# Two-layer graph network on one core: one-hots of rows and columns made two steps ahead, and 40 gathered blocks in layer 1 instead of 46

## The chip, the cores and the metric

One core of one Trainium2 chip runs the whole program. The metric is the device time of one execution in microseconds (us). The five engines are named as in the profile: PE (TensorE, with its weight loads as PEld), DVE (VectorE), ACT (ScalarE), POOL (GpSimd) and SP (SyncE, which only issues DMAs here).

## The reference

The graph has 12500 nodes of 128 features and 412500 edges (`src`, `dst`, a type of 0 or 1), sorted by `dst`. Each of two layers normalizes and rectifies the nodes, sums neighbours' rows by destination, multiplies by small weights and adds the result to `x`.

```python
h = jnp.maximum(_layernorm(x), 0.0)
# layer 0: m = h[src] @ W.T + b, W and b by the edge's type
x = x + relu(segment_sum(m, dst) + (h @ W_self.T + b_self))
h = jnp.maximum(_layernorm(x), 0.0)
# layer 1
agg = segment_sum((h @ W_in.T)[src], dst)
deg = segment_sum(1, dst)
x = x + agg + deg[:, None] * (h @ W_out.T)
```

## The kernel before

The kernel sums rows of `h` first and multiplies by the weights afterwards. A row of `h` is held as three bf16 parts (`RW` = 384 columns). Nodes are in `NB` = 98 blocks of 128; edges, sorted by destination, lie in tiles of 128. The sum for a block of destinations is made in one of two ways. The first `GATHERED[l]` blocks of layer l are gathered, the others, `D` of them, are dense.

A **gathered** block: for each tile of 128 edges POOL issues one indirect DMA that brings the 128 source rows from the table in HBM into `rows` (L578). DVE makes the one-hot matrix of destinations for a group of `GROUP` = 5 tiles (`make_hot`, L1128), and PE multiplies rows by one-hots into `bank_g` (`add_group`, L665). `rows` holds `RINGS` = 3 groups, so POOL waits for `s.added` of the group three before.

A **dense** block: the adjacency counts of 128 (layer 1) or 64 (layer 0) destinations against all 98 blocks of sources are built in 16 steps. In each step DVE makes a one-hot of source rows and one of source columns for a few edge slots of each destination (`mark`, L1140 and L1142), PE multiplies them (`build`, eight matmuls, L717) into `bank_m`, and ACT copies that pair of banks into the adjacency (`built`, two copies, L958) before PE may build the next step. Meanwhile PE multiplies the adjacency of the block before with the table in SBUF, 98 matmuls of 384 columns, 6 or 7 in a step (`dense`, L732). The edges of a dense block come by one indirect DMA from `pk` (POOL, L563), are unpacked on DVE (`unpack`, L1152 to L1175) and turned on PE (L683, L684). Layer 0 does this for all its 98 blocks, since it also counts edges so; layer 1 for its dense blocks only.

Each engine runs through the same loop over steps `s_` in program order, and `Plan` says what lies in which step. A layer has `S = 16 * (Q + 1)` steps for its Q dense units (Q = D in layer 1, 2 D in layer 0), and the groups are spread evenly over them:

```python
self.due = [8 + g * (self.S - 12) // self.groups for g in range(self.groups)]
```

Within one step PE adds the groups that are due, turns and finishes blocks (L675, L692, L705, L706), builds, and does its dense part; DVE makes the hots of groups due up to three steps later, then one pair of marks, then the rest of its work. The two one-hot buffers `is_row` and `is_col` are used in turn, and `mark` for step s+1 waits until both halves of the build of step s-1 are done (`s.built`). POOL does not run by steps: its queue is just the gathers in order, with the `pk` DMAs between the groups. Layer 1 starts when every block of layer 0 is stored (`s_stored`); SP then loads the new table into SBUF.

Of the kernel before, what the change touches and what calls it, by code (L numbers as in the profile page):

```python
# [4 lines left out]
P = 128  # L5


def gnn_kernel(nc, x, src, dst, etype, w_data, b_data, w_ctrl, b_ctrl, w_self, b_self, w_in, w_out, out):
    fp32, bf16, i32, i16 = mybir.dt.float32, mybir.dt.bfloat16, mybir.dt.int32, mybir.dt.int16
# [6 lines left out]
    NB = -(-N // P)  # L16
# [20 lines left out]

    GATHERED = (NB * 29 // 49 // 2 * 2, NB * 23 // 49 // 2 * 2)  # L40
    KINDS = (2, 1)
    GROUP, RINGS = 5, 3
    PACKS = 4


    WIN, LEAD = 96, 46
# [20 lines left out]
    class Plan:  # L67


        def __init__(self, l):  # L70
            self.G = G = GATHERED[l]
            self.D = NB - G
# [76 lines left out]
    with ctx:  # L149
        def sb(name, shape, dt):  # L150
            return ctx.enter_context(nc.sbuf_tensor(name, shape, dt))

        def pb(name, shape, dt=fp32):
            return ctx.enter_context(nc.psum_tensor(name, shape, dt))

        def sem(name):
            return ctx.enter_context(nc.semaphore(name))
# [15 lines left out]
        ROWS_AT = 2 * A_W  # L173
        HOT_AT = ROWS_AT + RINGS * GROUP * RW // 2
        R_AT = HOT_AT + RINGS * GROUP * WIN
        C_AT = R_AT + 2 * 4 * P // 2
        CW = max(2 * NC0, 4 * NC1)
        PACK_AT = C_AT + 2 * CW // 2
        V_AT = PACK_AT + PACKS * 3 * P
        E_AT = V_AT + 3 * HALF  # L180
        GE_AT = E_AT + HALF
# [6 lines left out]
        arena = sb("arena", [P, max(D16_AT + (T + 1) // 2, RC_AT + 4 * P)], fp32)  # L188
# [9 lines left out]
        adj1 = [a.rearrange("p (c d) -> p c d", d=P) for a in adj]  # L198
        rows = arena[:, ROWS_AT:HOT_AT].bitcast(bf16).rearrange("p (t c) -> p t c", c=RW)
        hot = arena[:, HOT_AT:R_AT].bitcast(bf16).rearrange("p (t c) -> p t c", c=2 * WIN)  # L200
        is_row = arena[:, R_AT:C_AT].bitcast(bf16).rearrange("p (k n r) -> p k n r", k=2, n=4)
        is_col = arena[:, C_AT:PACK_AT].bitcast(bf16).rearrange("p (k c) -> p k c", k=2)
        pack = arena[:, PACK_AT:V_AT].rearrange("p (k c) -> p k c", k=PACKS)
        mine = arena[:, V_AT:E_AT].rearrange("p (k s) -> p k s", k=3)
        slot = arena[:, E_AT:GE_AT].bitcast(i32)
# [13 lines left out]

        ident = sb("ident", [P, P], fp32)  # L220
        ident_b = sb("ident_b", [P, P], bf16)
        ones = sb("ones", [P, 1], fp32)
        ones_b = sb("ones_b", [P, 1], bf16)
        eps = sb("eps", [P, 1], fp32)
        offset = sb("offset", [P, 1], fp32)
        base_g = sb("base_g", [P, 1], fp32)
        wT = sb("wT", [P, 5, F], fp32)
        bias = sb("bias", [P, 3, F], fp32)
        count = sb("count", [P, 3, NB], fp32)
# [4 lines left out]
        tmax = sb("tmax", [P, CH], fp32)  # L234
        tmin = sb("tmin", [P, CH], fp32)
        worst = sb("worst", [P, 4], fp32)
        missed = sb("missed", [P, 1], fp32)
        covered = sb("covered", [1, 1], i32)
        root = sb("root", [P, 1], fp32)


        SG_AT = 0
# [30 lines left out]
        shift = arena2[:, LN_AT + 4 * NB:LN_AT + 5 * NB]  # L273
        st1 = sb("st1", [P, 6], fp32)
        mv1 = sb("mv1", [P, 2], fp32)
        std1 = sb("std1", [P, 1], fp32)
        rstd1 = sb("rstd1", [P, 1], fp32)
        shift1 = sb("shift1", [P, 1], fp32)

        def stat_col(c, a, b):  # L280
            return stats.rearrange("p (n c) -> p n c", c=6)[:, a:b, c]
# [4 lines left out]
        bank_m = [pb(f"bank_m{k}", [P, 512]) for k in range(2)]  # L286
# [6 lines left out]
        iota_r = iota_ps[:, 0:P]  # L293
# [47 lines left out]
        for l in range(2):  # L341
            s = Layer()
# [3 lines left out]
            s.pair_out = sem(f"l{l}_pair_out")  # L346
            s.pack = [sem(f"l{l}_pack{k}") for k in range(PACKS)]
            s.unpacked = sem(f"l{l}_unpacked")
# [145 lines left out]
        def _(pool):  # L494
# [60 lines left out]
            def fast(l):  # L555
# [3 lines left out]
                def fetch(i):  # L559
                    if i >= PACKS:  # L560
                        pool.wait_ge(s.unpacked, i - PACKS + 1)
                    m = plan.fetch[i][1]
                    pool.indirect_dma_start(  # L563
                        out=pack[:, i % PACKS, :], out_offset=None, in_=pk,
                        in_offset=bass.IndirectOffsetOnAxis(ap=list_at[:, m:m + 1], axis=0),
                        compute_op=ALU.bypass).then_inc(s.pack[i % PACKS], 16)
# [45 lines left out]
        def _(pe):  # L612
            pe.wait_ge(s_ident, 2)
            pe.wait_ge(s_w, 16 * 8)
            for j in range(5):
                last = pe.transpose(turned[j // 4][:, j % 4 * P:(j % 4 + 1) * P], w_raw[:, j, :], ident[:, :])
# [21 lines left out]
            for c in range(CH):  # L638
                last = pe.matmul(centre[:, c:c + 1], base[0:1, c * P:(c + 1) * P], ones[0:1, 0:1],
                                 start=(c == 0), stop=(c == CH - 1), skip_group_check=True)  # L640
            last.then_inc(s_centre, 1)
            pe.wait_ge(s_extent, 2)
            for c0 in range(0, CH, 4):
                pe.wait_ge(s_trc, g - 3)
                for c in range(c0, min(c0 + 4, CH)):
                    last = pe.matmul(turned[g % 4][:, (c - c0) * P:(c - c0 + 1) * P],
                                     tmax[:, c:c + 1].to_broadcast([P, P]), ident[:, :], start=True, stop=True)
# [60 lines left out]
            def build(l, s_):  # L708
                plan, s = plans[l], L[l]
                pe.wait_ge(s.marks, s_ + 1)  # L710
                if s_ > 0:
                    pe.wait_ge(s.adj, s_)
                nc_ = (NC0, NC1)[l]
                for n in range(plan.at_once):
                    for hf in range(2):
                        at = slice(hf * HALF, (hf + 1) * HALF)
                        last = pe.matmul(bank_m[hf][:, n * nc_:(n + 1) * nc_], is_row[at, s_ % 2, n, :],  # L717
                                         is_col[at, s_ % 2, n * nc_:(n + 1) * nc_], start=True, stop=True)
                        if n == plan.at_once - 1:
                            last.then_inc(s.built, 1)  # L720

# [298 lines left out]
        def _(dve):  # L1020
# [111 lines left out]
            def mark(l, s_):  # L1132
                plan, s = plans[l], L[l]
                n, nc_ = plan.at_once, (NC0, NC1)[l]
                i, pr = s_ // (16 * plan.sub), s_ % (16 * plan.sub) * n
                if pr == 0:
                    dve.wait_ge(s.turn_out, plan.turn["list", plan.G + i] + 1)
                if s_ >= 2:
                    dve.wait_ge(s.built, 2 * s_ - 2)
                dve.tensor_tensor(is_row[:, s_ % 2, 0:n, :], iota_r.unsqueeze(1).to_broadcast([P, n, P]),  # L1140
                                  rc[:, i % 2, 0, pr:pr + n].unsqueeze(2).to_broadcast([P, n, P]), op=ALU.is_equal)
                dve.tensor_tensor(is_col[:, s_ % 2, 0:n * nc_].rearrange("p (n c) -> p n c", n=n),  # L1142
                                  iota_c[l].unsqueeze(1).to_broadcast([P, n, nc_]),
                                  rc[:, i % 2, 1, pr:pr + n].unsqueeze(2).to_broadcast([P, n, nc_]),
                                  op=ALU.is_equal).then_inc(s.marks, 1)
# [32 lines left out]
            def sum_parts(l, q):  # L1178
                plan, s = plans[l], L[l]
                wait(dve, s.dense_out, q + 1)  # L1180
                after(dve.tensor_tensor(d_sum[:, 0, :], d_sb[:, F:2 * F], d_sb[:, 2 * F:3 * F], op=ALU.add), s.sum_d, q + 1)  # L1181
                if q > 0:
                    dve.wait_ge(s.turn, plan.turn["sum", q - 1] + 1)
                dve.tensor_tensor(d_sum[:, 1, :], d_sum[:, 0, :], d_sb[:, 0:F], op=ALU.add).then_inc(s.d_sum, 1)
# [42 lines left out]
            def fast(l):  # L1227
                plan, s = plans[l], L[l]
                g = done = 0
                if l == 1:  # L1230
                    dve.wait_ge(L[0].added, plans[0].groups)
                    dve.wait_ge(L[0].built, 32 * plans[0].Q)
                    dve.wait_ge(L[0].turn, len(plans[0].turn))
                for s_ in range(plan.begin, plan.stop):
                    while g < plan.groups and plan.due[g] <= s_ + 3:
                        make_hot(l, g)
                        g += 1
                    if 0 <= s_ + 1 < 16 * plan.Q:
                        mark(l, s_ + 1)
                    if plan.summed(s_) is not None:  # L1240
                        sum_parts(l, plan.summed(s_))
                    if s_ in plan.fetch_at:
                        done = unpack(l, plan.fetch_at[s_], done)
                    if s_ - 2 in plan.end_at:
                        q = plan.end_at[s_ - 2]
                        if q >= 2 and l == 0:
                            dve.wait_ge(s_stored[0][q % 2], 32 * (q // 2))
                        if q >= 2 and l == 1:
                            dve.wait_ge(s_stored[1][q % 2], 16 * (q // 2))
                        finish(l, q, q // 2, plan.end[q][1], q % 2, 0)  # L1250
                    if l == 0:
                        if s_ - 4 in plan.end_at:
                            finish_scale(plan.end_at[s_ - 4], 0)
                        if s_ - 6 in plan.end_at:
                            finish_rest(plan.end_at[s_ - 6], plan.end_at[s_ - 6] % 2, 0)
                        if s_ - 8 in plan.end_at:
                            finish_low(plan.end_at[s_ - 8], plan.end_at[s_ - 8] % 2, 0)
# [60 lines left out]
```

## Time and profile before

| | us |
|---|---|
| median of 3 runs | 4766.32 (4763.54 to 4766.8) |
| the profiled execution, its own time | 4766.91 |
| its span, first to last instruction | 4765.0 |
| busy: PE / POOL / DVE / ACT | 4086.7 / 3483.0 / 3366.0 / 2301.2 |
| mean granted TensorE clock | 0.951 |

Preparation ends at about 190 us, layer 0 runs to about 2765 us, and layer 1 to the end. Busy time on POOL is only the issuing instruction itself; the 0.30 us between two of its DMAs is put down as "issue". A share of 1.0 in the granted clock is 2.4 GHz, and the other level is 1.2 GHz.

### The profile page before, as it was taken

The page shows a single profiled execution, that of the slowest core. Times are in us where ns is not written, and L with a number is a line of the kernel's source. Part 1 is how long each engine was busy: PE and PEld are TensorE (multiplying, and loading weights), DVE is VectorE, ACT ScalarE, POOL GpSimd, SP SyncE. Part 2 cuts the span into 40 slices and gives each one's busy share as a digit, 9 for nine tenths or more (in the row PEclk, how much of TensorE's full clock was granted, in tenths as well). Part 3 has the DMA queues.
Part 4 walks back from the last instruction along what each step waited for, and adds up shares of the span by engine and source line. Part 5 has one row for each costly group of instructions (what it writes and reads, how often), then busy time and mean ns, then how long its engine had stood idle before and what let it go on. Part 6 is the DMA issues. An engine that isn't in the chain of part 4 may idle for free.

```text
span 4765.0 us, 104535 instructions
## 1 busy us (share of the span) xinstructions
PE 4086.7 (86%) x40877; PEld 2488.4 (52%) x40877; DVE 3366.0 (71%) x7696; ACT 2301.2 (48%) x5544; POOL 3483.0 (73%) x3682
## 2 busy tenths in 40 slices
PE   1399999999999999999999968888888888888887
PEld 0255555555555555555555535444545555554544
DVE  5677777778777777777777656666666666666664
ACT  4455555555555555555555434444444444444443
POOL 4377777777777777777777757777777777777776
PEclk7599999999999999999999979999999999999999
DMA  7233333333333333333333353333333333333332
GB/s 189 74 87 93 92 92 94 93 94 90 95 93 92 94 92 91 96 89 95 93 92 93 88 151 89 89 88 91 89 88 90 88 91 89 89 91 88 89 89 79
DMA packets 304713, 448.62 MB, mean 94 GB/s; under 512 B 76065, under 2 KB 239327, under 8 KB 304223
## 3 DMA queue, kind: packets, MB, share of 16 engines
q0 software_dynamic: 175488, 369.46, 29.0%
q1 hardware_dynamic: 121784, 66.09, 4.8%
q10 hardware_dynamic: 6951, 6.30, 0.5%
q8 instruction: 336, 5.51, 0.5%
q14 instruction: 154, 1.26, 0.1%
HBM read 404.39 MB, written 37.20 MB: 93 GB/s over the span
## 4 chain that ended last, share of the span: by engine, by line
POOL 46%; PE 28%; issue 16%; DVE 6%; ACT 3%; ACTq 1%; DMA 1%; POOLq 0%; DVEq 0%; SPq 0%
POOL arena L578 44%; PE bank_d L732 16%; PE bank_g L665 6%; PE bank_m L717 4%; POOL arena L563 2%; DVE arena L1142 1%; ACT arena L857 1%; DVE arena L1140 1%; ACT arena L958 1%; ACTq L819 1%; DVE arena L1128 0%; DMA arena<-table,idx 0%; ACT arena L894 0%; DVE arena L1032 0%; DVE tab L1051 0%
## 5 line engine op out<-in xcount | busy, mean ns | idle before, releaser
L578 POOL DMA_INDIRECT arena<-table,idx x3456 | 3274.3, 947 | 1062.6 <-issue 1044.8
L958 ACT ACTIVATE arena<-bank_m 128x392 bf16<-128x392 f32 x4224 | 1890.4, 501 | 1747.3 <-PE bank_m L717 1725.9
L732 PE MATMUL bank_d<-tab,arena 128*128 128x384 bf16 x12936 | 2535.4, 334 | 32.7 <-ACT arena L894 32.3
L1140 DVE TENSOR_TENSOR arena<-iota_ps,arena 128x256 bf16<-128x256 f32 (+1 forms) x2112 | 1109.6, 525 | 1113.1 <-PE bank_m L717 1093.3
L732 PEld LDWEIGHTS bank_d<-tab,arena 128*128 128x128 bf16 x12936 | 1114.1, 99 | 917.2 <-issue 298.9
L1142 DVE TENSOR_TENSOR arena<-iota_ps,arena 128x392 bf16<-128x392 f32 x2112 | 1170.9, 554 | 0.0
L665 PE MATMUL bank_g<-arena 128*128 128x192 bf16 (+15 forms) x14118 | 844.5, 213 | 334.0 <-DMA arena<-table,idx 332.9
L665 PEld LDWEIGHTS bank_g<-arena 128*128 128x128 bf16 x14118 | 772.0, 99 | 482.5 <-issue 395.3
L717 PE MATMUL bank_m<-arena 64*128 64x98 bf16 (+1 forms) x11776 | 755.4, 230 | 78.3 <-ACT arena L958 37.7
L717 PEld LDWEIGHTS bank_m<-arena 64*128 64x128 bf16 x11776 | 350.9, 96 | 585.3 <-DVE arena L1142 261.5
L1128 DVE TENSOR_TENSOR arena<-iota_ps,rel 128x960 bf16<-128x960 f32 (+2 forms) x692 | 641.6, 927 | 6.1 <-DVE mv L1207 0.5
L563 POOL DMA_INDIRECT arena<-pk,list_at x150 | 142.5, 950 | 105.3 <-issue 72.1
L926 ACT ACTIVATE arena<-bank_a 128x128 f32<-128x128 f32 x196 | 54.4, 277 | 202.9 <-PE bank_a L692 181.2
L917 ACT ACTIVATE arena<-bank_a 64x128 f32<-64x128 f32 x184 | 50.0, 272 | 173.3 <-PE bank_a L684 172.2
L1181 DVE TENSOR_TENSOR d_sum<-arena 128x128 f32<-128x128 f32 x132 | 38.8, 294 | 93.4 <-ACT arena L894 92.1
L531 POOL TENSOR_TENSOR arena<-arena,tab 128x256 f32<-128x256 f32 x49 | 35.4, 725 | 80.8 <-ACT tab L861 76.0
L683 PE MATMUL bank_a<-ident,arena 128*128 128x128 f32 x92 | 29.5, 321 | 74.2 <-DVE arena L1175 74.0
L894 ACT ACTIVATE arena<-bank_d 128x384 f32<-128x384 f32 x132 | 64.8, 491 | 48.9 <-PE bank_d L732 48.9
L627 PE MATMUL bank_m<-ident,arena 128*128 128x128 f32 x30 | 7.0, 407 | 79.1 <-ACT arena L843 39.8
L692 PE MATMUL bank_a<-ident_b,tab 128*128 128x128 bf16 x588 | 68.3, 228 | 6.5 <-ACT arena L917 4.9
L1152 DVE SCALAR_TENSOR_TENSOR arena<-arena,node 128x192 f32<-128x192 int32 x150 | 61.2, 408 | 15.8 <-DMA arena<-pk,list_at 15.8
L1051 DVE TENSOR_TENSOR tab<-arena,tab 128x256 bf16<-128x256 f32 x49 | 41.6, 866 | 33.1 <-ACT tab L874 32.9
(133 smaller groups left out, 1580.4 us busy)
## 6 DMA issues: line engine op xcount, KB each, us to landing
arena<-table,idx POOLq DMA_INDIRECT x3456
table<-tab SPq DMA_DIRECT2D x7, 1344.0 KB, 5.6
table<-arena SPq DMA_DIRECT2D x98, 96.0 KB
tab<-table SPq DMA_DIRECT2D x7, 1344.0 KB, 16.4
x<-arena SPq DMA_DIRECT2D x98, 64.0 KB
arena<-x SPq DMA_DIRECT2D x98, 64.0 KB
arena<-in_x_dram SPq DMA_DIRECT2D x97, 64.0 KB
out_dram<-arena SPq DMA_DIRECT2D x97, 64.0 KB
```

What stands on the lines that cost most here:

```text
L563: pool.indirect_dma_start(out=pack[:, i % PACKS, :], out_offset=None, in_=pk, in_offset=bass.IndirectOffsetOnAxis(ap=list_at[:, m:m + 1], ...
L578: pool.indirect_dma_start(out=rows[:, g % RINGS * GROUP + t % GROUP, :], out_offset=None, in_=tables[l], in_offset=bass.IndirectOffsetOnAx ...
L665: last = pe.matmul(bank_g[p % 2][:, to:to + (c1 - c0) * y], rows[:, at, a * F:(a + 1) * F], hot[:, at, c0 * y:c1 * y], start=(a == 0 and p ...
L692: last = pe.matmul(bank_a[:, 0:P], mine[:, a * F:(a + 1) * F], ident_b[:, :], start=(a == 0), stop=(a == 2))
L717: last = pe.matmul(bank_m[hf][:, n * nc_:(n + 1) * nc_], is_row[at, s_ % 2, n, :], is_col[at, s_ % 2, n * nc_:(n + 1) * nc_], start=True, ...
L732: last = pe.matmul(bank_d[:, 0:RW], adj[q % 2][:, b * P:(b + 1) * P], tab[:, b, :], start=(b == 0), stop=(b == NB - 1))
L894: act.activation(d_sb[:, :], bank_d[:, 0:RW], ACT.Copy).then_inc(s.dense_out, 1)
L958: last = act.activation((adj0, adj1)[l][q % 2][:, :, at:at + n], bank_m[hf][:, 0:n * nc_].rearrange("p (n c) -> p c n", n=n), ACT.Copy)
L1128: dve.tensor_tensor(hot[:, at:at + n, 0:c], iota_w[:, 0:c].unsqueeze(1).to_broadcast([P, n, c]), (rel0, rel1)[l][:, ts[0]:ts[0] + n].unsqu ...
L1140: dve.tensor_tensor(is_row[:, s_ % 2, 0:n, :], iota_r.unsqueeze(1).to_broadcast([P, n, P]), rc[:, i % 2, 0, pr:pr + n].unsqueeze(2).to_bro ...
L1142: dve.tensor_tensor(is_col[:, s_ % 2, 0:n * nc_].rearrange("p (n c) -> p n c", n=n), iota_c[l].unsqueeze(1).to_broadcast([P, n, nc_]), rc[ ...
L1152: after(dve.scalar_tensor_tensor(out=arena[:, V_AT:E_AT], in0=pack[:, k, 0:W3].bitcast(i32), scalar=node[:, m:m + 1], in1=pack[:, k, W3:2 ...
```

## The change

`mark` gets four buffers in place of two and is called for step s+2 in place of s+1, so that it waits for the build of step s-2 in place of s-1. `GATHERED[1]` falls from 46 to 40. To make room in SBUF, eight one-column tensors (`ones`, `eps`, `missed`, `root` and four others) become columns of one tensor `cells`, and `offset`, which nothing used, goes.

```diff
-    GATHERED = (NB * 29 // 49 // 2 * 2, NB * 23 // 49 // 2 * 2)
+    GATHERED = (NB * 29 // 49 // 2 * 2, NB * 20 // 49 // 2 * 2)
+    MARKS, AHEAD = 4, 2
...
-        C_AT = R_AT + 2 * 4 * P // 2
+        C_AT = R_AT + MARKS * 4 * P // 2
...
-        PACK_AT = C_AT + 2 * CW // 2
+        PACK_AT = C_AT + MARKS * CW // 2
...
-                        last = pe.matmul(bank_m[hf][:, n * nc_:(n + 1) * nc_], is_row[at, s_ % 2, n, :],
-                                         is_col[at, s_ % 2, n * nc_:(n + 1) * nc_], start=True, stop=True)
+                        last = pe.matmul(bank_m[hf][:, n * nc_:(n + 1) * nc_], is_row[at, s_ % MARKS, n, :],
+                                         is_col[at, s_ % MARKS, n * nc_:(n + 1) * nc_], start=True, stop=True)
...
-                if s_ >= 2:
-                    dve.wait_ge(s.built, 2 * s_ - 2)
-                dve.tensor_tensor(is_row[:, s_ % 2, 0:n, :], iota_r.unsqueeze(1).to_broadcast([P, n, P]),
+                if s_ >= MARKS:
+                    dve.wait_ge(s.built, 2 * (s_ - MARKS) + 2)
+                dve.tensor_tensor(is_row[:, s_ % MARKS, 0:n, :], iota_r.unsqueeze(1).to_broadcast([P, n, P]),
...
-                    if 0 <= s_ + 1 < 16 * plan.Q:
-                        mark(l, s_ + 1)
+                    if 0 <= s_ + AHEAD < 16 * plan.Q:
+                        mark(l, s_ + AHEAD)
```

In layer 1 the number of gathered tiles goes from 1530 to 1332, of groups from 306 to 267, of matmuls in `add_group` from 6240 to 5421, of dense blocks from 52 to 58, and of steps `S` from 848 to 944. Layer 0 keeps 1926 tiles, 386 groups, 98 `pk` DMAs and 1296 steps.

POOL's queue at the start of layer 1 is this before (L563 is the DMA from `pk`, L578 a gather of one tile):

```order
L563 DMA arena<-pk,list_at 128x384 x2
L578 DMA arena<-table,idx 128x384 x20
L563 DMA arena<-pk,list_at 128x384
L578 DMA arena<-table,idx 128x384 x30
L563 DMA arena<-pk,list_at 128x384
L578 DMA arena<-table,idx 128x384 x30
```

and this in the changed kernel, whose lines are numbered one higher:

```order
L564 DMA arena<-pk,list_at 128x384 x2
L579 DMA arena<-table,idx 128x384 x15
L564 DMA arena<-pk,list_at 128x384
L579 DMA arena<-table,idx 128x384 x25
L564 DMA arena<-pk,list_at 128x384
L579 DMA arena<-table,idx 128x384 x25
```

Between two `pk` DMAs, that is in one dense block's 16 steps, stand 20 to 25 gathers in place of mostly 30.

DVE's queue at the first steps of layer 1, from the first one-hot of rows (L1140, with L1142 for the columns; L1128 is the hot of a group), is this before:

```order
L1140 TENSOR_TENSOR arena<-iota_ps,arena 128x512 [waits l1_turn_out]
L1142 TENSOR_TENSOR arena<-iota_ps,arena 128x392
L1140 TENSOR_TENSOR arena<-iota_ps,arena 128x512
L1142 TENSOR_TENSOR arena<-iota_ps,arena 128x392
L1140 TENSOR_TENSOR arena<-iota_ps,arena 128x512 [waits l1_built]
L1142 TENSOR_TENSOR arena<-iota_ps,arena 128x392
```

and this in the changed kernel:

```order
L1141 TENSOR_TENSOR arena<-iota_ps,arena 128x512 [waits l1_turn_out]
L1143 TENSOR_TENSOR arena<-iota_ps,arena 128x392
L1141 TENSOR_TENSOR arena<-iota_ps,arena 128x512
L1143 TENSOR_TENSOR arena<-iota_ps,arena 128x392
L1141 TENSOR_TENSOR arena<-iota_ps,arena 128x512
L1143 TENSOR_TENSOR arena<-iota_ps,arena 128x392
L1141 TENSOR_TENSOR arena<-iota_ps,arena 128x512
L1143 TENSOR_TENSOR arena<-iota_ps,arena 128x392
L1141 TENSOR_TENSOR arena<-iota_ps,arena 128x512 [waits l1_built]
```

Four pairs go ahead without a wait for a build in place of two.

PE's queue around step 16 of layer 1, where its dense part begins, is this before (L717 build, L665 group, L732 dense):

```order
L665 MATMUL bank_g<-arena 128x96 x15
L717 MATMUL bank_m<-arena 128x98 x24
L665 MATMUL bank_g<-arena 128x96 x15
L717 MATMUL bank_m<-arena 128x98 x8
L732 MATMUL bank_d<-tab,arena 128x384 x6
L717 MATMUL bank_m<-arena 128x98 x8
L732 MATMUL bank_d<-tab,arena 128x384 x6
L665 MATMUL bank_g<-arena 128x96 x15
```

and this in the changed kernel:

```order
L666 MATMUL bank_g<-arena 128x96 x15
L718 MATMUL bank_m<-arena 128x98 x24
L733 MATMUL bank_d<-tab,arena 128x384 x6
L718 MATMUL bank_m<-arena 128x98 x8
L733 MATMUL bank_d<-tab,arena 128x384 x6
L666 MATMUL bank_g<-arena 128x96 x15
```

The fourth group moved from step 16 to step 18; from here on a group stands every 3.54 steps in place of every 2.77.

## Rows read from the trace of the kernel before

**Rows 1.** Busy time by stretch: layer 0, and layer 1.

```profile
core 0: us, PE busy (x) PEld busy (x) DVE busy (x) ACT busy (x) POOL busy (x), PEclk, DMA share, GB/s
200.00:2732.00 2532.00, 2410.97 (x21752) 1455.11 (x21753) 1963.12 (x4840) 1370.31 (x3298) 1912.19 (x2017) 0.99 0.34 92
...
2765.00:4748.00 1983.00, 1612.54 (x18754) 982.05 (x18754) 1270.39 (x2574) 832.98 (x1987) 1496.92 (x1582) 0.93 0.35 94
```

**Rows 2.** Waits of POOL in layer 0: us in total, times, longest.

```profile
POOL arena L578 <- PE bank_g L665: 13.3, 25, 2.4
```

**Rows 3.** Waits of POOL in layer 1.

```profile
POOL arena L563 <- DMA x<-arena: 33.2, 1, 33.2
POOL arena L578 <- PE bank_g L665: 4.5, 1, 4.5
```

**Rows 4.** POOL's instructions in order of time: first and last of each layer.

```profile
190.67 1.19 POOL L563 DMA_INDIRECT arena<-pk,list_at  x1 [27.06 <-issue]
...
2731.21 0.94 POOL L578 DMA_INDIRECT arena<-table,idx  x1 [0.30 <-issue]
2765.33 0.94 POOL L563 DMA_INDIRECT arena<-pk,list_at  x1 [33.18 <-DMA x<-arena]
...
4747.41 0.95 POOL L578 DMA_INDIRECT arena<-table,idx  x1 [0.30 <-issue]
```

**Rows 5.** Waits of PE in layer 1.

```profile
PE bank_g L665 <- DMA arena<-table,idx: 320.9, 221, 3.9
```

**Rows 6.** Waits of PE's weight loads in layer 0.

```profile
PEld bank_m L717 <- DVE arena L1142: 240.5, 544, 1.7
```

**Rows 7.** PE in layer 1 in order of time, clock full.

```profile
2848.88 0.35 PE L717 MATMUL bank_m<-arena 64*128 64x98 bf16 x8
...
2850.33 0.36 PE L717 MATMUL bank_m<-arena 64*128 64x98 bf16 x8
2850.62 1.15 PE L732 MATMUL bank_d<-tab,arena 128*128 128x384 bf16 x6
2851.61 1.06 PE L665 MATMUL bank_g<-arena 128*128 128x86 bf16 x30
2852.60 0.35 PE L717 MATMUL bank_m<-arena 64*128 64x98 bf16 x8
...
2854.31 0.35 PE L717 MATMUL bank_m<-arena 64*128 64x98 bf16 x8
```

**Rows 8.** The same, a group of 15 matmuls with a block's finish behind it.

```profile
4700.09 0.80 PE L665 MATMUL bank_g<-arena 128*128 128x96 bf16 x15 [1.00 <-DMA arena<-table,idx]
4700.73 0.45 PE L705 MATMUL bank_b<-wT,arena 128*128 128x128 f32 x2
4701.02 0.39 PE L706 MATMUL bank_b<-wT,arena 128*128 128x128 f32 x2
4701.33 0.35 PE L717 MATMUL bank_m<-arena 64*128 64x98 bf16 x8
```

**Rows 9.** The same, after a long wait for a gather.

```profile
3361.55 1.08 PE L665 MATMUL bank_g<-arena 128*128 128x90 bf16 x30 [2.63 <-DMA arena<-table,idx]
...
3364.41 0.51 PE L717 MATMUL bank_m<-arena 64*128 64x98 bf16 x8
3364.85 2.09 PE L732 MATMUL bank_d<-tab,arena 128*128 128x384 bf16 x6
3366.87 0.36 PE L717 MATMUL bank_m<-arena 64*128 64x98 bf16 x8
```

**Rows 10.** ACT between two builds of layer 1.

```profile
4703.19 0.89 ACT L958 ACTIVATE arena<-bank_m 128x392 bf16<-128x392 f32 x2 [0.55 <-PE bank_m L717]
```

**Rows 11.** Grouped by line: gathers, one-hots of columns (layer 0), gathers (layer 1).

```profile
L578 POOL DMA_INDIRECT arena<-table,idx x1920 | 1820.7, 948 | 590.6 <-issue 577.3 <-PE bank_g L665 13.3
...
L1142 DVE TENSOR_TENSOR arena<-iota_ps,arena 128x392 bf16<-128x392 f32 x1278 | 708.6, 554 | 0.0
...
L578 POOL DMA_INDIRECT arena<-table,idx x1530 | 1447.9, 946 | 470.2 <-issue 465.8 <-PE bank_g L665 4.5
```

## What the time will be

> **What bounds the kernel now.** I began with busy time by stretch [rows 1]. In layer 0 PE is busy for 2411 of 2532 us and in layer 1 for 1613 of 1983, while POOL shows only 75% in both. That 75% misleads. POOL's waits say why: beside the 0.30 us between two DMAs it waits for almost nothing, for PE 25 times and 13.3 us in all of layer 0 [rows 2], and once, 4.5 us, in layer 1 [rows 3]. So POOL issues without a stop. Its period follows from the first and last DMA of layer 1 [rows 4]: 4747.41 - 2765.33 = 1982.1 us, less the 4.2 us by which the one wait exceeds 0.30, over 1581 intervals (1582 DMAs, 1530 gathers and 52 from pk) gives **1.251 us**. Layer 0 has 2024 DMAs, and 2023 intervals in 2540.5 us give 1.256. Both layers last as long as POOL needs to issue its DMAs.
>
> PE is a close second in layer 0 and far behind in layer 1. There it waits 320.9 us for gathers, 221 times [rows 5]. Of layer 0's 25 waits on PE, 25 times 0.30 or 7.5 us is the usual gap, so only 5.8 us are real. In layer 0 PE's weight loads for the builds wait 240.5 us for the one-hot of columns [rows 6], but since POOL is not held up, this costs almost nothing: PE uses up slack of the three groups in `rows`.
>
> **The change part by part.** *Fewer gathers.* Layer 1 drops 1530 - 1332 = 198 gathers and adds 6 DMAs from pk, each of which takes POOL as long as a gather: 192 fewer. At 1.251 us this is **-240.2 us**, if POOL stays the bound. POOL then needs 1390 x 1.251 = 1739 us for layer 1, and the question is whether PE can do its larger part in that.
>
> *PE's work in layer 1 after.* I price it by steps at full clock. A plain step is 1.45 us (2848.88 to 2850.33), one with a group of 30 matmuls 2.27 (2850.33 to 2852.60), so +0.82; one that turns a list is 1.71 (2852.60 to 2854.31), +0.26 [rows 7]. A group of 15 takes 0.64 until the next thing starts, and a finish 0.60 (4700.09, 4700.73, 4701.33) [rows 8]. A plain step can't be shorter: ACT copies the pair of banks for 0.89 us between two builds [rows 10], and 0.35 for the build and the hand-overs come on top. The change leaves that loop as it is. In a step with a group this wait is covered, so 15 matmuls add some 0.56 rather than 0.64. The mean group after has 5421 / 267 = 20.3 matmuls, between 15 and 30 by a third: 0.65 us. The sum: 944 x 1.45 = 1369; 267 x 0.65 = 174; 98 blocks turned and finished, at most 0.60 + 0.1 each, 69; 58 lists and sums at 0.3, 17. Together **1629 us**, 110 us or 6% under POOL's 1739.
>
> The same prices give for the kernel before 848 x 1.45 + 306 x 0.65 + 69 + 16 = 1514 us. With the 321 us of waiting that makes 1835 of 1983; 148 us are left over. Most of them are slow steps after long waits: behind a wait of 2.63 us a plain step takes 2.46 us instead of 1.45 (3364.41 to 3366.87) [rows 9], with the matmuls at the spacing of 1.2 GHz, and the granted clock of layer 1 is 0.93 against 0.99 in layer 0, where PE has no such waits [rows 1]. After the change the mean wait per group falls from 321 / 306 = 1.05 us to 110 / 267 = 0.41, so I expect few of these steps. If PE fell behind, the waits and with them the slow steps would go, and `rows` lends it three groups. That is the state of layer 0 now. The Trainium skill (TensorE: Matmul & The Clock Gate, "HAM oscillation — how this bites in real kernels") says that waits for DMA put the array back to half clock and that the penalty is paid again at each wait; the trace agrees, and by that rule the extra goes with the waits. I take POOL as the bound.
>
> *Marks two steps ahead.* This takes DVE's delay out of PE's builds, up to 240.5 us of weight-load waits in layer 0 [rows 6]. It is worth at most what POOL waits for PE there, 5.8 us [rows 2], since nothing else shortens POOL's queue. Some of that is the fill of the rings before PE's first group, which no mark shortens. I take **-3 us**, bounds 0 and -7 with a little for the tail, where PE lags the last gather. The longer lead costs DVE nothing: all its work was 1270 us for 848 steps, 1.50 a step [rows 1]; 944 steps at that price are 1414, 81% of 1739, about its share in layer 0 (1963 of 2532). Queued behind the moved pair are a group's hot (made up to three steps early already), the sum of a dense block, the unpacking of the next list and the finish. Each is taken up in the same step as before, with one more pair of marks in stock.
>
> *Hand-over and ends.* The 33.2 us in which POOL waits for the last store of layer 0 [rows 3] stay. In layer 1's first steps POOL still waits 4.5 us for the first group, due at step 8 as before; the next ones are due at 11, 14, 18 and 21 instead of 10, 13, 16 and 18, at most three steps or 4.4 us later, which POOL's lead over them covers. At the end 8 steps lie behind the last group's due step (936 to 944) instead of 7 (841 to 848): **+1 us**. The moved columns cost nothing: each is read by the same instructions, one column as before.
>
> Sum: -240.2 - 3 + 1 = -242 us. The profiled execution took 4766.9 us (span 4765.0), half a microsecond over the median of 4766.3. So 4766.3 - 242 = 4524, and I say **4525 us**.
>
> **The rivals.** *PE becomes the bound* (0.18). If the 148 us left over are not slow clock but a cost of each step, they grow with the steps to 148 x 944 / 848 = 165, and PE needs 1629 + 165 = 1794 us, 55 more than POOL: 4580. If half of them stay, PE needs 1711, which is less than POOL's 1739, and only unevenness shows. For it speaks that PE's busy time alone was 1613 us [rows 1]; against it that this time holds slow matmuls. The middle of this case is 4555.
>
> *The forecast, but layer 0 gives nothing or more* lies within the forecast's own range of 4518 to 4542 (0.77 for the case). That is also where it ends if marks ahead do nothing at all: 4528. *Much more from layer 0* (0.01) would need POOL to issue faster than 1.251 us, for which no row speaks.
>
> *The new cover doesn't come about and layer 1 runs at POOL's period with gaps* (0.02): if POOL is stopped at each ring by 0.4 us, 267 groups cost 107 us: 4632.
>
> *Slower than before* (0.02): DVE's denser one-hots hold up POOL's issue. DVE's share in layer 1 rises from 1270 / 1983 = 64% to some 80%. If each DMA lost half of one 0.55 us one-hot [rows 11], 0.28 us on 1390 DMAs is 389 us: 4914. It decides from 240.2 / 1390 = 0.17 us a DMA. Against it: a gather takes 948 ns in layer 0, where DVE is busy 78% of the time, and 946 in layer 1 at 64% [rows 11]. That 2 ns is 3 us over layer 1. The Trainium skill (SBUF — State Buffer, "SBUF: two separate sides") warns that a VectorE instruction in a two-port mode locks GpSimd out of the port by which it writes DMA descriptors; the trace does not bear it out for these one-hots.
>
> **How the numbers follow.** The likeliest case gives 4525. The range has to reach into the case in which PE is the bound: its lower half, to 4562. On the low side the whole of layer 0's 5.8 us and a shorter tail give 4518, with room for what a run differs 4514. So 4514 to 4562. A measurement here tells 0.2%, some 10 us, from no change. Only the last rival and a mishap of its size end above 4757: slower 0.02, same 0.01, faster 0.97.
>
> **What would show it.** Right: in the profile after, layer 1 lasts near 1743 us from POOL's first to last DMA, POOL's period stays 1.25, its waits for PE stay under 10 us in each layer, PE's waits for gathers in layer 1 fall from 321 to some 110 us, the granted clock there rises to 0.97 or more, and the weight loads' wait for L1142 (L1143 after) in layer 0 all but goes. Wrong: POOL waits for PE by tens of us in layer 1 (PE is the bound), or gathers above 960 ns or gaps above 0.30 us (DVE in POOL's way). If PE's waits for gathers stay above 200 us while POOL's period holds, my prices for PE's steps were too high, with no harm to the time.

## The result and the profile after

The changed kernel takes **4525.35 us** (median of 4, 4524.61 to 4534.47) against 4765.51 before; the ratio is 0.9501, 95% interval 0.9484 to 0.9517. The forecast was 4525, with a range of 4514 to 4562.

The profiled execution is the longest of the four, 4534.47 us (span 4532.2). Busy time by stretch, layer 0 and layer 1, columns as in [rows 1]:

```profile
200.00:2734.00 2534.00, 2410.55 (x21758) 1453.19 (x21759) 1954.32 (x4845) 1367.43 (x3298) 1917.11 (x2016) 0.99 0.33 92
...
2767.00:4513.00 1746.00, 1613.50 (x19295) 989.06 (x19296) 1357.02 (x2775) 924.33 (x2200) 1319.95 (x1390) 0.98 0.34 96
```

PE is busy for the same 1613 us of layer 1 as before [rows 1]. Its work is not the same: 58 dense blocks in place of 52, and 267 groups in place of 306, which by the prediction's prices is 1629 us of steps in place of 1514. The stretch is 237 us shorter, so PE's share rises from 81% to 92%, and the granted clock from 0.93 to 0.98. The same kinds of matmul take less time each. The dense ones show it in the groups by line of layer 1, whose columns are those of [rows 11]: 329 ns in the mean (L733), where they had 343 before (L732).

```profile
L579 POOL DMA_INDIRECT arena<-table,idx x1332 | 1264.9, 950 | 408.4 <-issue 405.5 <-PE bank_g L666 3.0
...
L733 PE MATMUL bank_d<-tab,arena 128*128 128x384 bf16 x5730 | 1096.6, 329 | 15.0 <-ACT arena L895 15.0
...
L732 PE MATMUL bank_d<-tab,arena 128*128 128x384 bf16 x5053 | 1027.5, 343 | 11.9 <-ACT arena L894 11.5 <-issue 0.4
```

POOL's instructions in order of time, to be set beside [rows 4]:

```profile
2734.19 0.95 POOL L579 DMA_INDIRECT arena<-table,idx  x1 [0.30 <-issue]
2766.97 0.95 POOL L564 DMA_INDIRECT arena<-pk,list_at  x1 [31.82 <-DMA x<-arena]
...
4511.81 0.95 POOL L579 DMA_INDIRECT arena<-table,idx  x1 [0.30 <-issue]
```

Layer 1 runs from POOL's first to last DMA in 4511.81 - 2766.97 = 1744.8 us, against 1982.1. Now the waits. POOL's in layer 0 and, under the dots, in layer 1 [rows 2, 3]:

```profile
POOL arena L579 <- PE bank_g L666: 5.2, 9, 2.4
...
POOL arena L579 <- PE bank_g L666: 3.0, 2, 2.6
```

PE's for gathers in layer 1 [rows 5]:

```profile
PE bank_g L666 <- DMA arena<-table,idx: 79.4, 105, 2.3
```

and the weight loads' in layer 0 [rows 6]:

```profile
PEld bank_m L718 <- DVE arena L1143: 137.5, 303, 1.5
```

Within each layer POOL is still never stopped for long. PE's waits for gathers fell from 320.9 to 79.4 us, and their longest from 3.9 to 2.3.

### The profile page after: what moved, and what is told of

The parts are those of the page before. It is cut to its first block, busy times and chain, and to the rows that moved or that the text cites. A ratio compares the mean times of both kernels' runs of the same rounds, so it can differ in the third digit from the quotient of the medians.

```text
span 4532.2 us, 105965 instructions
## 1 busy us (share of the span) xinstructions
PE 4088.7 (90%) x41432; PEld 2493.3 (55%) x41432; DVE 3443.0 (76%) x7897; ACT 2389.6 (53%) x5757; POOL 3311.5 (73%) x3490
## 4 chain that ended last, share of the span: by engine, by line
POOL 62%; issue 21%; PE 9%; DVE 4%; ACT 2%; ACTq 1%; DMA 1%; POOLq 0%; DVEq 0%; SPq 0%
POOL arena L579 59%; PE bank_d L733 5%; POOL arena L564 3%; PE bank_g L666 2%; PE bank_m L718 1%; ACT arena L858 1%; ACTq L820 1%; DVE arena L1143 1%; DVE arena L1141 0%; ACT arena L959 0%; DVE arena L1033 0%; DVE tab L1052 0%; ACT tab L875 0%; DMA arena<-table,idx 0%; DMA arena<-pk,list_at 0%
## 5 line engine op out<-in xcount | busy, mean ns | idle before, releaser
L579 POOL DMA_INDIRECT arena<-table,idx x3258 | 3096.7, 950 | 998.1 <-issue 989.9
L959 ACT ACTIVATE arena<-bank_m 128x392 bf16<-128x392 f32 x4416 | 1976.2, 501 | 1596.7 <-PE bank_m L718 1546.2
L733 PE MATMUL bank_d<-tab,arena 128*128 128x384 bf16 x13524 | 2584.2, 328 | 35.8 <-ACT arena L895 35.8
L733 PEld LDWEIGHTS bank_d<-tab,arena 128*128 128x128 bf16 x13524 | 1146.8, 98 | 916.7 <-issue 252.3
L1141 DVE TENSOR_TENSOR arena<-iota_ps,arena 128x256 bf16<-128x256 f32 (+1 forms) x2208 | 1172.1, 531 | 428.5 <-PE bank_m L718 394.4
L1143 DVE TENSOR_TENSOR arena<-iota_ps,arena 128x392 bf16<-128x392 f32 x2208 | 1226.1, 555 | 0.0
L666 PE MATMUL bank_g<-arena 128*128 128x192 bf16 (+15 forms) x13299 | 797.7, 213 | 121.9 <-DMA arena<-table,idx 116.5
L666 PEld LDWEIGHTS bank_g<-arena 128*128 128x128 bf16 x13299 | 732.6, 98 | 250.2 <-issue 155.2
L1200 DVE SCALAR_TENSOR_TENSOR arena<-bias,count,bank_b 128x128 f32<-128x128 f32 x98 | 33.9, 346 | 100.1 <-issue 96.4
L1196 DVE TENSOR_TENSOR arena<-bank_b,arena 128x128 f32<-128x128 f32 x98 | 28.3, 289 | 65.3 <-issue 53.0
L684 PE MATMUL bank_a<-ident,arena 128*128 128x128 f32 x98 | 28.8, 294 | 46.8 <-DVE arena L1176 46.6
```

What stands on the lines that cost most here:

```text
L579: pool.indirect_dma_start(out=rows[:, g % RINGS * GROUP + t % GROUP, :], out_offset=None, in_=tables[l], in_offset=bass.IndirectOffsetOnAx ...
L666: last = pe.matmul(bank_g[p % 2][:, to:to + (c1 - c0) * y], rows[:, at, a * F:(a + 1) * F], hot[:, at, c0 * y:c1 * y], start=(a == 0 and p ...
L733: last = pe.matmul(bank_d[:, 0:RW], adj[q % 2][:, b * P:(b + 1) * P], tab[:, b, :], start=(b == 0), stop=(b == NB - 1))
L959: last = act.activation((adj0, adj1)[l][q % 2][:, :, at:at + n], bank_m[hf][:, 0:n * nc_].rearrange("p (n c) -> p c n", n=n), ACT.Copy)
L1141: dve.tensor_tensor(is_row[:, s_ % MARKS, 0:n, :], iota_r.unsqueeze(1).to_broadcast([P, n, P]), rc[:, i % 2, 0, pr:pr + n].unsqueeze(2).to ...
L1143: dve.tensor_tensor(is_col[:, s_ % MARKS, 0:n * nc_].rearrange("p (n c) -> p n c", n=n), iota_c[l].unsqueeze(1).to_broadcast([P, n, nc_]), ...
```

## The experiments

All are variants of the changed kernel; each ratio is to the kernel before on the same chip. In all but one of them only three numbers differ: `GATHERED`, `MARKS` (one-hot buffers) and `AHEAD` (steps that a pair is made ahead). They are written below as (`MARKS`, `AHEAD`): (4, 2) are the new marks, (2, 1) the old ones.

### One part alone: the marks

```diff
-    GATHERED = (NB * 29 // 49 // 2 * 2, NB * 20 // 49 // 2 * 2)
+    GATHERED = (NB * 29 // 49 // 2 * 2, NB * 23 // 49 // 2 * 2)
```

> One part alone: four one-hot buffers made two steps ahead, 46 gathered blocks in layer 1 as before. Theory A (POOL's queue of DMAs is the bound in both layers, PE has slack): nothing to gain but what POOL waits for PE in layer 0, so -1 to -6 us against before, 4760 to 4765, and layer 1 from POOL's first to last DMA stays at 1982 us. Theory B (the marks ahead are what made the kernel faster): a gain of tens of us, 4700 or less. In both the weight loads' wait for the one-hot of columns in layer 0 falls from 240.5 us to about 140.

Measured: 4764.16 us against 4766.29, ratio 0.9996 (0.9986 to 1.0005). The weight loads' wait in layer 0 fell to 136.6 us. The gain of 2 us lies in the noise of the timing, but it has a place in the profile: what POOL waits for PE in layer 0 beyond the usual 0.30 us falls from 5.8 to 3.3 us. In the other profiles with 58 gathered blocks in layer 0 the same sum is 2.4 to 2.9 us with four buffers (five of them) and 3.9 and 4.6 with two, at PE's usual clock and with the list turned at its old step. Taking 104 us of waiting from PE's weight loads moved the end by 2. Theory A.

### The other part alone: fewer gathers

```diff
-    MARKS, AHEAD = 4, 2
+    MARKS, AHEAD = 2, 1
```

> The other part alone: 40 gathered blocks, with two one-hot buffers made one step ahead. Theory A (PE has some 80 us to spare in layer 1 even when it sometimes waits for DVE): -235 us, 4528 to 4535, POOL waits for PE under 10 us in layer 1. Theory B (with a hot of a group in front, a pair of one-hots takes DVE 1.7 us against PE's step of 1.45, and the list's unpacking 1.9 more, so that PE loses some 140 us in 267 groups and 58 lists): PE is the bound, 1629 + 140 = 1769 us in layer 1, total 4550 to 4565, and POOL waits for PE by 25 us or more.

Measured: 4528.15 us, ratio 0.9499 (0.9483 to 0.9515). POOL waits for PE in layer 1 five times:

```profile
POOL arena L579 <- PE bank_g L666: 4.8, 5, 3.1
```

So the fewer gathers alone bring 238 of the 240 us. What the marks add at 40 blocks can't be told from nothing: the ratios with and without them are 0.9501 and 0.9499. At 40 gathered blocks PE has enough to spare to hide whatever the old marks cost it. Theory A again; my 140 us of cost in theory B was far too high, as the next runs show.

### 38 blocks, with new and with old marks

```diff
-    GATHERED = (NB * 29 // 49 // 2 * 2, NB * 20 // 49 // 2 * 2)
+    GATHERED = (NB * 29 // 49 // 2 * 2, NB * 19 // 49 // 2 * 2)
```

> All of the change, but 38 gathered blocks in layer 1. POOL then needs 1326 x 1.251 + 3 = 1662 us for layer 1 and PE by the prices of the prediction 976 x 1.45 + 254 x 0.65 + 69 + 18 = 1667 us. Theory A (these prices hold and PE's slack at 40 was real): PE and POOL are level, some 10 to 35 us of unevenness on top, total 4450 to 4485. Theory B (PE is already the bound at 40, its slack a mirage of short waits): each 32 more steps cost more than 66 fewer gathers give, total 4530 or more. The granted clock of layer 1 should reach 0.99.

> 38 gathered blocks with two one-hot buffers made one step ahead. If the lead of the marks is worth something only where PE is the bound, it shows here: theory A says 60 to 140 us slower than the same with four buffers, 4540 to 4600. If DVE's delay costs PE nothing there either, within 10 us of it.

Measured: 4456.52 us with four buffers, ratio 0.9349 (0.9334 to 0.9365), **69 us faster than the changed kernel**; 4474.94 with two, ratio 0.9389 (0.9374 to 0.9405). Between the two lie 18 us. That is more than the 2 to 3 us between the medians at 46 and at 40 blocks, and it fits neither expectation, 60 to 140 us or at most 10. The profiled execution of the first, at a granted clock of 0.655, is not among these numbers; the last section has it.

> The kernel with 38 gathered blocks once more, for a profile in which the granted clock is not held at 0.65 throughout. Theory A: total 4456 again; in layer 1 PE's waits for gathers are under 40 us, POOL's waits for PE beyond 0.30 us add to 5 to 20 us, since the two are level, and the granted clock is 0.99 or more.

Measured: 4457.14 us, ratio 0.935 (0.9334 to 0.9366). Busy time in layer 1:

```profile
2763.00:4426.00 1663.00, 1613.37 (x19382) 1004.43 (x19383) 1381.71 (x2836) 951.23 (x2264) 1255.51 (x1325) 0.99 0.36 97
```

and POOL's waits in it:

```profile
POOL arena L579 <- PE bank_g L666: 4.8, 3, 2.6
```

PE no longer shows a single wait for a gather from 2806 to 4430 us, and POOL is stopped only 3 times, for 3.9 us beyond the usual gap (I had expected 5 to 20): the two are level, at 97% PE. POOL's first to last DMA takes 1663.1 us, where 1326 DMAs at 1.251 and the start gave 1662. Against the second profile of the changed kernel, further down, that is 78 us less, of which 8 are lost again behind POOL's last DMA, where PE has more left to do: 29.1 us in place of 20.6.

### 36 blocks: where PE takes over

```diff
-    GATHERED = (NB * 29 // 49 // 2 * 2, NB * 20 // 49 // 2 * 2)
+    GATHERED = (NB * 29 // 49 // 2 * 2, NB * 18 // 49 // 2 * 2)
```

> All of the change, but 36 gathered blocks in layer 1. POOL needs 1262 x 1.251 + 3 = 1582 us there, PE by the prices of the prediction 1008 x 1.45 + 240 x 0.65 + 69 + 19 = 1706 us. Theory A (PE's prices hold, PE is now the bound alone): layer 1 takes 1706 us and up to 15 more, total 4490 to 4510, some 35 to 50 us more than with 38 blocks (4456.5). Theory B (PE's price for a dense block is lower than I put it, since plain steps can be shortened where PE never waits for a gather): as fast as with 38 or faster, 4460 or less.

Measured: 4494.45 us, ratio 0.9428 (0.9413 to 0.9444), 38 us slower than with 38 blocks. POOL's waits in layer 1:

```profile
POOL arena L579 <- PE bank_g L666: 175.9, 166, 3.3
```

From first to last DMA layer 1 takes 4463.88 - 2761.12 = 1702.8 us, where the prices of the prediction gave PE 1706. This is the direct test of those prices, since here PE alone decides. Taken from PE itself, from its first build of the layer to the end of its last dense matmul, it is 1712.9 us, 7 more than the prices say.

### 56 blocks in layer 0

```diff
-    GATHERED = (NB * 29 // 49 // 2 * 2, NB * 20 // 49 // 2 * 2)
+    GATHERED = (NB * 28 // 49 // 2 * 2, NB * 20 // 49 // 2 * 2)
```

> All of the change with 40 blocks in layer 1, and 56 gathered blocks in layer 0 instead of 58. POOL loses 66 gathers there, 82.6 us. PE gets 64 more steps of 1.45, 93 us, less 14 groups of some 1.15, 16 us, so 77 more. Theory A (PE is as full as POOL in layer 0: it waits for gathers for 36 of 2532 us): PE becomes the bound, 30 to 45 us slower than with 58, 4555 to 4570. Theory B (layer 0 has slack as layer 1 had): faster than 4525 by tens of us.

Measured: 4572.01 us (4568.96 to 4577.02), ratio 0.9591 (0.9575 to 0.9607), 47 us slower than the changed kernel. The same step to fewer gathers that pays in layer 1 costs in layer 0. POOL's waits in layer 0:

```profile
POOL arena L579 <- PE bank_g L666: 179.4, 155, 5.3
```

The cost is 2 us above my range. One part that the estimate left out is on record: PE waits 19.9 us for the lists in layer 0, where the changed kernel has 7.9.

### Buffers or order?

```diff
-    MARKS, AHEAD = 4, 2
+    MARKS, AHEAD = 4, 1
```

> 38 gathered blocks, four one-hot buffers, but each pair made one step ahead in DVE's order as in the old kernel. It tells the buffers from the order. Theory A (what counts is how far DVE may run ahead, which the buffers set: four pairs in stock either way): within 6 us of four buffers made two steps ahead, 4456 to 4463. Theory B (what counts is that the pair stands ahead of the hot, the list and the dense sum in DVE's queue): most of the 18 us between old and new marks is lost again, 4468 to 4475.

Measured, with 38 blocks: 4456.81 us, ratio 0.9351 (0.9336 to 0.9367). Nothing of the 18 us is lost, so the pair need not stand ahead of the rest in DVE's queue. That left the number of pairs in stock, which I tested with three buffers:

```diff
-    MARKS, AHEAD = 4, 2
+    MARKS, AHEAD = 3, 2
```

> 38 gathered blocks, three one-hot buffers, two steps ahead. DVE then waits for the build of the same step as in the old kernel, but has one pair more in stock. Theory A (the stock decides, and one pair more covers a hot: 0.6 + 1.07 = 1.7 us of DVE against two PE steps of 1.45): most of the 18 us comes back, 4457 to 4463. Theory B (it takes the full four, because a list's unpacking, 1.9 + 1.07 us, outlasts two steps): 4464 to 4472.

Measured: 4475.83 us, ratio 0.939 (0.9375 to 0.9406), as slow as with two. **Both my theories fell**: one pair more in stock is worth nothing. What the runs have in common is the build for which DVE waits before step s of its program: that of s-1 with (2, 1) and (3, 2), of s-2 with (4, 2), of s-3 with (4, 1). So DVE's lead in its whole program counts, and the question is which of its other products PE waits for.

### What PE waits for

PE's steps of the 38-block kernels between 2800 and 4440 us, sorted by what they hold, differ in one class only. The steps that turn a dense block's list and nothing else take 1.59 us in the mean (34 of them) with (4, 2), 1.96 (34) with (2, 1) and 1.96 (34) with (3, 2); plain steps take 1.47 to 1.48 in all three. With those that hold a list and other work besides there are 58 list steps. Their sum is 110.3 us with (4, 2) and with (4, 1), and 126.3 us with (2, 1) and with (3, 2). That difference of 16.0 us is all by which layer 1 differs between them: from POOL's first to last DMA 1663.1 and 1662.9 us against 1679.1 and 1679.4. Here is such a step with the old marks, DVE and PE in order of time:

```profile
3033.70 0.69 DVE L1141 TENSOR_TENSOR arena<-iota_ps,arena 128x512 bf16<-128x512 f32 x1 [0.24 <-PE bank_m L718]
3034.31 0.56 DVE L1143 TENSOR_TENSOR arena<-iota_ps,arena 128x392 bf16<-128x392 f32 x1
3034.73 0.36 PE L718 MATMUL bank_m<-arena 64*128 64x98 bf16 x8
3034.78 0.41 DVE L1153 SCALAR_TENSOR_TENSOR arena<-arena,node 128x192 f32<-128x192 int32 x1
...
3036.22 0.29 DVE L1176 CAST arena<-arena 128x256 f32<-128x256 int32 x1
...
3036.57 0.33 PE L684 MATMUL bank_a<-ident,arena 128*128 128x128 f32 x1 [0.40 <-DVE arena L1176]
3036.73 0.27 PE L685 MATMUL bank_a<-ident,arena 128*128 128x128 f32 x1
3036.94 0.35 PE L718 MATMUL bank_m<-arena 64*128 64x98 bf16 x8
```

and the same block's with four buffers:

```profile
3030.70 0.35 PE L718 MATMUL bank_m<-arena 64*128 64x98 bf16 x8
3030.90 0.41 DVE L1153 SCALAR_TENSOR_TENSOR arena<-arena,node 128x192 f32<-128x192 int32 x1
...
3032.14 0.36 PE L718 MATMUL bank_m<-arena 64*128 64x98 bf16 x8
3032.24 0.44 DVE L1176 CAST arena<-arena 128x256 f32<-128x256 int32 x1
...
3033.41 0.27 PE L684 MATMUL bank_a<-ident,arena 128*128 128x128 f32 x1
3033.52 0.27 PE L685 MATMUL bank_a<-ident,arena 128*128 128x128 f32 x1
3033.72 0.35 PE L718 MATMUL bank_m<-arena 64*128 64x98 bf16 x8
```

With old marks DVE may unpack the list only after a pair that itself waited for PE's last build. The unpacking ends at 3036.5 and PE, which wants the list one step later, stands still; build to build takes 2.21 us. With four buffers DVE begins one build earlier and has the list ready at 3032.7, and the step takes 1.58. The last run puts this to the test from the other side: old marks, but PE and ACT turn the list one step later.

```diff
-                if s - 1 in self.fetch_at and self.fetch[self.fetch_at[s - 1]][1] >= G:
-                    self.turn["list", self.fetch[self.fetch_at[s - 1]][1]] = len(self.turn)
+                if s - 2 in self.fetch_at and self.fetch[self.fetch_at[s - 2]][1] >= G:
+                    self.turn["list", self.fetch[self.fetch_at[s - 2]][1]] = len(self.turn)
...
-                    if s_ - 1 in plan.fetch_at and plan.fetch[plan.fetch_at[s_ - 1]][1] >= plan.G:
-                        turn_list(l, plan.fetch_at[s_ - 1])
+                    if s_ - 2 in plan.fetch_at and plan.fetch[plan.fetch_at[s_ - 2]][1] >= plan.G:
+                        turn_list(l, plan.fetch_at[s_ - 2])
```

(and the same for `turned_list` on ACT)

> 38 gathered blocks and the old marks (two buffers, one step ahead); PE and ACT turn a dense block's list two steps after DVE's step that unpacks it, in place of one. With old marks the steps that turn a list took 1.97 us, with four buffers 1.59, and PE waited there for the last instruction of the unpacking. Theory A (this wait is what the four buffers take away, because DVE may run further ahead and unpacks earlier): the 18 us come back without any new buffer, 4456 to 4462. Theory B (the marks themselves come late for the builds): nothing changes, 4472 to 4477.

Measured: 4468.37 us, between the two ranges. On this chip the kernel before took 4775.80 in place of some 4766, so the number doesn't compare as it stands; the ratio is 0.9356 (0.934 to 0.9371), against 0.9349 and 0.935 with four buffers and 0.9389 with two. The ratio may flatter it: the kernel before is bound by POOL throughout, and this one is not. PE's own stretch of layer 1, from the first build to the end of the last dense matmul, holds no wait for a gather in any of these kernels: 1680.4 us here, 1690.7 with the old marks and 1673.8 with four buffers. So 10 of 17 us are back, without a buffer. PE's waits for the list (L684 for L1176) are gone from the list of waits from 2806 to 4430 us, where the old marks had this:

```profile
PE bank_a L684 <- DVE arena L1176: 9.8, 28, 0.7
```

and POOL's waits for PE in layer 1 fell from 36.6 us, 48 times, to this:

```profile
POOL arena L579 <- PE bank_g L666: 12.2, 16, 2.9
```

The 58 list steps take 114.5 us. The rest does not come back because a small wait takes the list's place: PE waits 8.3 us, 30 times, for the pair of one-hots that stands behind the unpacking. So theory A holds for the larger part, and four buffers remove both waits.

### The changed kernel again

> The changed kernel itself once more. Its profiled execution took 4534.5 us and the three others 4524.6 to 4526.0; in the profiled one POOL's period was 1.254 us in place of 1.251. Theory A (that execution differed, not the kernel): 4525 again, and a period of 1.251 in its profile. Theory B (more one-hots on DVE stretch POOL's period): 1.254 again.

Measured: 4526.83 us, ratio 0.9494 (0.9478 to 0.951). In its profile layer 1 takes 4504.88 - 2763.64 = 1741.2 us. POOL waits for PE 4 times, 4.1 us, of which 2.9 lie beyond the usual gap; that leaves 1738.3 us for 1389 intervals, 1.2515 each. Theory A: the 1.254 of the first profile belonged to that execution.

## Why the prediction was right

- **POOL is the bound in both layers: right.** -240.2 us was the term for 192 DMAs at 1.251. In the second profile of the changed kernel layer 1 shrank by 1982.1 - 1741.2 = 240.9 us, and the fewer gathers alone gave 238 in the medians.
- **PE has 110 us to spare: right in kind, too much in size.** It waited 79.4 us for gathers (75.4 in the second profile), of which the prediction expected "some 110". The sum of its prices was right, which the 36-block kernel showed (1706 expected, 1702.8 measured); single terms were less so: with 38 blocks a step with only a list takes 1.59 us and one with only a sum 1.74, together 0.43 over two plain steps, where the prediction had 0.3. What the 110 us left out is the slow steps of the next point.
- **The slow steps go with the waits: borne out.** The granted clock rose to 0.98 (1.00 from 2806 us on with 36 blocks), and the dense matmuls became 4% shorter in the mean. The prediction had 148 us of layer 1 left over beside PE's prices and 321 us of waits. By the same reckoning 1744.8 - 1629 - 79.4 = 36 us are left over in the changed kernel, and none at 36 blocks (1702.8 against 1706), where PE never waits for a gather. So the remainder shrinks with the waits. The rival, in which it grows with the steps to 165 us, did not come.
- **Marks ahead, -3 us: right within the noise, and the reason incomplete.** Alone they moved the end by 2 us. The prediction took the weight loads' wait for one-hots in layer 0 as what they remove and said that it "all but goes". It fell only from 240.5 to 137.5 us, and why so much is left stays open. And where PE is the bound, the lead helps by the lists that DVE unpacks earlier, which the prediction had priced at nothing.
- **The ends: the term of +1 us was too small.** In the second profile the tail behind POOL's last DMA took 4525.5 - 4504.9 = 20.6 us against 17.6, so +3. PE now comes late to its last group. It adds it 4.3 us after POOL issued the last DMA and without a wait, where it stood waiting for it before and added it 2.8 us after; the other 1.5 us lie behind the group. The last DMA and the last group, in the second profile and, under the dots, before:

```profile
4504.88 0.95 POOL L579 DMA_INDIRECT arena<-table,idx  x1 [0.30 <-issue]
4509.20 0.29 PE L666 MATMUL bank_g<-arena 128*128 128x6 bf16 x6
...
4750.17 0.51 PE L665 MATMUL bank_g<-arena 128*128 128x18 bf16 x15 [2.64 <-DMA arena<-table,idx]
```

- **DVE in POOL's way: did not come.** DVE was busy for 1357 of 1746 us in layer 1, 78%, and with 38 blocks for 83%. A gather took 947 or 948 ns in the profiles of all experiments but one. The exceptions are the first profile of the changed kernel and that of the later list, both 950; the same kernel had 948 in its second profile, so DVE's share does not explain them.
- **4525 against 4525.35 is luck in its last 2 us.** The sum of the terms was -242 us and the measured change -240.2. The kernel before ran 0.8 us faster beside this run than the 4766.3 that the forecast starts from, and 4524.3 had been rounded up to 4525.

## What to carry to other kernels

Where a number splits work between two engines, look for the value at which both are level; here it was the best of those tried. Both prices can be read from one trace: the period of the one that never waits, and the steps of the other in the stretches in which it doesn't. Read so, the trace of the kernel before already gave 38 blocks (1662 us against 1667) and not 40. When buffers are added, don't ask only what waits for their content: a wait for a free buffer holds back everything behind it in that engine's program, and the gain may lie with another product, as here with the list.

## What the runs showed of the hardware

The period of POOL's indirect DMAs is not the same in each run. From 350 to 2700 us, in layer 0, its mean was 1.2530 us in the profile of the kernel before, 1.2558 in the first profile of the changed kernel, and 1.2556 in the run with the later list, on whose chip the kernel before took 4775.8 us. Over 3400 DMAs that is the 9 or 10 us by which those runs stand out. With the later list all seven executions of the kernel before were slower, 4770.4 to 4777.5 us; with the changed kernel it was one execution of four, the others taking 4524.6 to 4526.0. So a kernel bound by such DMAs should be compared on one chip, and over several executions. What sets the period stays open.

One execution of the 38-block kernel ran with a granted clock of 0.65 wherever the other profiles show 1.0, and took 5660.7 us in place of 4456.5. That is neither of the two levels of the other profiles. A dense matmul took 416 ns in the mean, PE was busy for 95% of the span, and POOL waited for it 355 times, 814.8 us, in layer 0 and 237 times, 547.3 us, in layer 1. One such execution was seen, and what brings it about stays open.
